# Turning the quantised weights on TensorE during attention instead of turning them in the DMA load

## The reference

```python
x = x + _L0_xattn_ref(_layernorm(x, axis=-1), ctx_768, Wq, Wk, Wv, Wo, bo)      # 8 heads of 64
x = x + _L0_ffn_ref(_layernorm(x, axis=-1), clip_x, clip_down, w_gate, w_up, w_down)

def _act_fake_quant(x, clip_factor):          # one scale for the whole tensor
    scale = jax.nn.sigmoid(clip_factor) * jnp.max(jnp.abs(x)) / 127.0
    return jnp.clip(round(x / scale), -128.0, 127.0) * scale
def _weight_fake_quant(w):                    # one scale for each row
    scale = jnp.max(jnp.abs(w), axis=1, keepdims=True) / 127.0
    return jnp.clip(round(w / scale), -128.0, 127.0) * scale
xq = _act_fake_quant(x, clip_x[0])
gate = xq @ _weight_fake_quant(w_gate).T      # w_gate, w_up: 1408 x 512
up = xq @ _weight_fake_quant(w_up).T
h = _act_fake_quant(silu(gate) * up, clip_down[0])
return h @ _weight_fake_quant(w_down).T       # w_down: 512 x 1408
```

## Time and profile before

| | |
|---|---|
| median of 3 runs | 570.46 us (569.67 to 570.75) |
| the profiled execution | 570.46 us, span of its profile 568.6 us |
| PE busy | 543.0 us, 95% |
| DVE busy | 471.8 us, 83% |
| ACT busy | 310.4 us, 55% |
| POOL busy | 233.9 us, 41% |
| DMA moved | 90.16 MB, mean 159 GB/s |

### The profile page before, as it was taken

One profiled execution on the slowest core, in us unless ns is written; L12 is line 12 of the kernel. 1 busy time (PEld: TensorE's weight loads), 2 busy tenths in 40 slices (PEclk: granted clock), 3 DMA queues, 4 the chain that ended last, 5 costly groups with the idle time before them and its releaser, 6 DMA issues.

```text
span 568.6 us, 8277 instructions
## 1 busy us (share of the span) xinstructions
PE 543.0 (95%) x2811; PEld 360.7 (63%) x2811; DVE 471.8 (83%) x874; ACT 310.4 (55%) x436; POOL 233.9 (41%) x352
## 2 busy tenths in 40 slices
PE   4999889999999999999899899999999999899997
PEld 2978678787888878787668544444444446443443
DVE  2747888989989888998987689889888988879883
ACT  3743546556464755544342666666666643999300
POOL 3576758679595968856342000000000000054442
PEclk9999999999999999999999999999999999999999
DMA  8708365756657573633295917541020010299887
GB/s 309 256 38 277 107 196 171 249 168 207 214 178 231 194 249 115 215 118 126 73 317 189 261 62 278 203 148 47 29 75 1 0 38 1 100 339 217 118 107 119
DMA packets 67779, 90.16 MB, mean 159 GB/s; under 512 B 32049, under 2 KB 34865, under 8 KB 67481
## 3 DMA queue, kind: packets, MB, share of 16 engines
q1 hardware_dynamic: 63413, 81.77, 44.6%
q0 software_dynamic: 4320, 7.87, 9.3%
q10 hardware_dynamic: 4, 0.00, 0.0%
HBM read 47.51 MB, written 37.78 MB: 150 GB/s over the span
## 4 chain that ended last, share of the span: by engine, by line
PE 50%; issue 34%; DVE 8%; DMA 5%; ACT 1%; POOL 1%; SPq 0%; POOLq 0%; DVEq 0%
PE QO L194 6%; PE QO L196 6%; PE QO L195 6%; PE SP L382 5%; PE WOP L495 4%; PE WOP L493 4%; PE WOP L494 4%; DMA out<-n2b 2%; PE PTP L1082 2%; PE PTP L430 2%; PE QO L1082 2%; PE SP L1082 2%; DMA wkr<-in_xattn_Wk 2%; PE MI L1082 1%; PE WOP L1082 1%
## 5 line engine op out<-in xcount | busy, mean ns | idle before, releaser
L45 POOL DMA_DIRECT2D out<-n2b x30 | 30.2, 1039 | 219.1 <-DVE n2b L1093 219.1
L977 PE MATMUL QO<-nT,wgu 128*128 128x512 bf16 x352 | 90.3, 379 | 0.6 <-ACT nT L221 0.6
L977 PE MATMUL SP<-nT,wgu 128*128 128x512 bf16 x352 | 90.3, 379 | 0.0
L983 ACT ACTIVATE sil<-QO,fsc 128x512 f32<-128x512 f32 x88 | 60.5, 687 | 50.7 <-PE QO L977 45.4
L987 DVE SCALAR_TENSOR_TENSOR h<-SP,fsc,sil 128x512 f32<-128x512 f32 x88 | 65.9, 749 | 14.9 <-PE SP L977 14.7
L422 POOL TENSOR_TENSOR PN<-P,rs 128x512 f32<-128x512 f32 x64 | 44.2, 712 | 57.8 <-DVE rs L414 57.8
L405 ACT ACTIVATE P<-P,r 128x616 f32<-128x616 f32 x32 | 26.0, 812 | 69.5 <-DVE P L401 69.5
L990 DVE TENSOR_REDUCE hmx<-h 128x1 f32<-128x512 f32 x88 | 60.4, 686 | 3.0
L977 PEld LDWEIGHTS SP<-nT,wgu 128*128 128x128 bf16 x352 | 34.4, 98 | 41.5
L977 PEld LDWEIGHTS QO<-nT,wgu 128*128 128x128 bf16 x352 | 33.2, 98 | 35.4 <-ACT nT L221 0.7
L194 PE MATMUL QO<-xTs,wqs 128*128 128x512 f32 x128 | 52.0, 407 | 1.8 <-DVE xTs L225 1.3
(11 more groups left out here) (169 smaller groups left out, 1162.9 us busy)
## 6 DMA issues: line engine op xcount, KB each, us to landing
xTr<-in_xT SPq DMA_DIRECT2D x8, 1024.0 KB, 8.0
xn<-in_x SPq DMA_DIRECT2D x32, 256.0 KB, 3.8
out<-x SPq DMA_DIRECT2D x32, 256.0 KB, 2.9
n_rows<-n SPq DMA_DIRECT2D x32, 256.0 KB, 2.6
n2b<-n_rows SPq DMA_DIRECT2D x32, 256.0 KB, 4.2
out<-n2b POOLq DMA_DIRECT2D x30, 256.0 KB, 4.4
h_spill<-h SPq DMA_DIRECT2D x2, 2816.0 KB, 9.3
h<-h_spill SPq DMA_DIRECT2D x6, 768.0 KB, 7.8
```

The costliest lines, as they stand in the source:

```text
L977: m = e.matmul(ps, wv_[:, k, col:col + 128], nT[:, b % 2, k, :], start=(k == 0), stop=(k == 3))
L983: t_sil[n] = add("act", lambda e: e.activation(sil[:, n % SR, :], gp, ACT.Silu, scale=fsc[:, ic:ic + 1]), [t_g[n], t_fs, t_h.get(n - SR)] ...
```

## The change

The weights are turned by TensorE during attention, and the two loads become plain ones.

- GpSimd's `wint` has one buffer where it had two, so `w_integer(i)` waits for the turning of tile i-1.
- `w_turn(i)` is new: TensorE transposes the 4 blocks of a tile (11 of a large one) into MI, in bf16; blocks 8 to 10 of a large tile go into the second bank of PTP. It waits for `w_integer(i)`, for the copy of the tile before (`t_we["last"]`), and for a large tile for the last reader of PTP.
- `w_out(i)` is new: ScalarE copies the turned blocks from PSUM to `wstg` (two buffers), in one instruction for a small tile and two for a large one; SP stores `wstg` to `wgud` or `wdd`, which now have the layout of `wgu` and `wd`. A store consists of 512 (large: 1408) pieces of 256 bytes, where it had 128 pieces of 1024 (2816) bytes.
- Tile i is turned at step i+2: a small one at the end of the step (before the query share that closes a step with t = 3), a large one, always at a step with t = 2, between `wo` and `PT`.
- The ring `P` of the softmax has 2 buffers where it had 3.
- The load of `wgu` is a plain DMA, added after step 31; the load of `wd` stays where it is and is plain.

```diff
-        wgud = dram("wgu_ints", (2 * I, D), bf16)
-        wdd = dram("wd_ints", (D, I), bf16)
+        wgud = dram("wgu_ints", (128, 4, 2 * I), bf16)
+        wdd = dram("wd_ints", (128, NI, D), bf16)
...
-        UR = 3
+        UR = 2
...
-        wint = sb(late, "wint", [128, 2, I], bf16)
+        wint = sb(late, "wint", [128, I], bf16)
+        wstg = sb(late, "wstg", [128, 2, NI, 128], bf16)
...
+            t_wb[i] = add("pool", lambda e: e.tensor_scalar(wint[:, 0:n * 128], v, -MAGIC, 1.0, ALU.add,
+                                                            ALU.mult), [t_wy[i], t_wt.get(i - 1)], "w_int")
+        MIb = MI[:, :].bitcast(bf16)
+        PTb = PTP[:, :].bitcast(bf16)
+        def w_turn(i, n):
+            nb = w_row(i)[1]
+            dst = [(MIb if k < 8 else PTb)[:, (k if k < 8 else k + 2) * 128:][:, 0:128] for k in range(nb)]
+            def fn(e):
+                for k in range(nb):
+                    m = e.transpose(dst[k], wint[:, k * 128:k * 128 + 128], identB[:, :])
+                return m
+            t_wt[i] = add("pe", fn, [t_wb[i], t_idB, t_we.get("last")] + ([t_pl[n - 1]] if nb > 8 else []),
+                          "w_tr")
+        def w_out(i, n, part):
+            nb = w_row(i)[1]
+            src, k0, k1, t = ((MIb[:, 0:1024], 0, min(nb, 8), None),
+                              (PTb[:, 1280:1664], 8, nb, t_PT.get(n) if nb > 8 else None))[part]
+            t_we["last"] = add("act", lambda e: e.activation(
+                wstg[:, i % 2, k0:k1, :], src[:, 0:(k1 - k0) * 128].rearrange("p (k c) -> p k c", c=128),
+                ACT.Copy), [t_wt[i], t, t_ws.get(i - 2)], "w_ev")
+            if part == 1:
+                return
+            at = W_ORDER[i]
+            out_ = wgud[:, :, at * 128:at * 128 + 128] if at < 22 else wdd[:, :, (at - 22) * 128:(at - 21) * 128]
+            t_ws[i] = dma("sp", out_, wstg[:, i % 2, 0:nb, :], [t_we["last"]], f"st_w{i % 2}")
...
+            if on["turn"] and not big:
+                w_turn(s - 2, s)
+                w_out(s - 2, s, 0)
...
-            t = add("pe", fn, t_dgs, "sd_mm")
+            t = add("pe", fn, [*t_dgs, t_we["last"]], "sd_mm")
...
-                t_wgu = c.dma_turn(wgu[:, :].rearrange("p (k n) -> p k n", k=4), wgud,
-                                   [t_qh[7, 3], t_ws[24], t_ws[25]], "ld_wgu")
             if s == 31:
-                gone = [t_S[31], t_q[7]]
+                gone = [t_S[31], t_q[7], t_ws[24], t_ws[25]]
+                t_wgu = dma("sp", wgu[:, :], wgud.rearrange("p k n -> p (k n)"), gone, "ld_wgu")
...
-        t_wdl = c.dma_turn(wd[:, :, :], wdd, flown + [t_g1, t_sdb, t_ws[24], t_ws[25]], "ld_wd")
+        t_wdl = dma("sp", wd[:, :, :], wdd, flown + [t_g1, t_sdb, t_ws[24], t_ws[25]], "ld_wd")
```

More of the change, by code:

```diff
@@ L37, in dma @@
         return self.add(engine, lambda e: e.dma_start(out, in_), waits, sig, 16)
-    def dma_turn(self, out, in_, waits, sig):
-        return self.add("sp", lambda e: e.dma_start_transpose(out, in_), waits, sig, 16)
     def dma_add(self, out, in_, waits, sig):
@@ L155, in block_kernel @@
         qs = sb(late, "qs", [128, 2, 4, 512])
-        wint = sb(late, "wint", [128, 2, I], bf16)
+        wint = sb(late, "wint", [128, I], bf16)
+        wstg = sb(late, "wstg", [128, 2, NI, 128], bf16)
         vbd = sb(late, "vbd", [128, 2, 5, 128], f32r)
         wraw = sb(late, "wraw", [128, 2, I])
-        sb(late, "unused1", [128, 88])
         os_ = sb(late, "os", [128, 2, 4, 512], f32r)
@@ L555, in block_kernel @@
         wd_v = w_down.rearrange("(r p) n -> r p n", p=128)
-        t_wr, t_wy, t_wb, t_ws, t_wiv = [Tokens() for _ in range(5)]
+        t_wr, t_wy, t_wb, t_wt, t_we, t_ws, t_wiv = [Tokens() for _ in range(7)]
+        t_we["last"] = None
         W_ORDER = [*range(22)]
@@ L595, in w_integer @@
             v = wraw[:, i % 2, 0:n * 128]
-            t_wb[i] = add("pool", lambda e: e.tensor_scalar(wint[:, i % 2, 0:n * 128], v, -MAGIC, 1.0, ALU.add,
-                                                            ALU.mult), [t_wy[i], t_ws.get(i - 2)], "w_int")
-            r = W_ORDER[i]
-            out_ = wgud[r * 128:r * 128 + 128, :] if r < 22 else wdd[(r - 22) * 128:(r - 21) * 128, :]
-            t_ws[i] = dma("sp", out_, wint[:, i % 2, 0:n * 128], [t_wb[i]], f"st_w{i % 2}")
+            t_wb[i] = add("pool", lambda e: e.tensor_scalar(wint[:, 0:n * 128], v, -MAGIC, 1.0, ALU.add,
[23 more added lines that the diff above has]
+            t_ws[i] = dma("sp", out_, wstg[:, i % 2, 0:nb, :], [t_we["last"]], f"st_w{i % 2}")
         for k in range(3):
@@ L650, in attend @@
             on = {"s": s + 1 < NT, "x": s + 3 < NT, "wo": s >= 5, "n2": s >= 6, "am": s >= 7, "w": 1 <= s < 27,
-                  "pv": t == 0 and b >= 1}
+                  "turn": 2 <= s < 28, "pv": t == 0 and b >= 1}
+            big = on["turn"] and w_row(s - 2)[1] > 8
             def when(key, fn, *args):
@@ L661, in turned @@
             def turned():
+                if big:
+                    w_turn(s - 2, s)
                 PT(s)
+                if big:
+                    w_out(s - 2, s, 1)
                 PT_high(s)
+                if big:
+                    w_out(s - 2, s, 0)
             if s < 26 and s != 2:
```

## The result

The changed kernel takes 577.96 us (median of 4 runs, 577.78 to 578.28); before, run beside it, takes 570.29 us (4 runs, 569.67 to 570.75). The ratio is 1.0125, with a 95% interval of 1.0106 to 1.0142: slower by 7.7 us. The profiled execution took 576.65 us (span 574.7), against 570.46 (span 568.6) before: 6.1 us longer in span. The four are on the high side: over all 21 executions of the changed kernel on record beside this result, the profiled one among them, the median is 577.57 us (575.74 to 578.86), some 7.3 us over before.

The account below looks back on a forecast made before the run. The prediction took TensorE to bound the kernel from 77 to 259 us. It added 7.6 us of paid turnings to 570.46 and took off 0.46 for a hole: 577.6 us, range 574.6 to 583.6.

Parts of the forecast that it names:

- 0.055 us of surcharge a tile: Attention: half of the 0.10 to 0.11 us by which f32 matmuls start slower behind a turning, added per tile.
- 18 small tiles are paid: Attention, tiles 2 to 23: 18 small tiles at 0.22 + 0.055 lengthen the kernel by 4.95 us.
- -0.46 for the hole at 208.68: TensorE's only hole between 77 and 259 us, behind an xn load, vanishes as TensorE is later: -0.46 us.
- Tiles 0, 1, 24 and 25 are hidden: Turned before 77 us or behind 259 us, ahead of TensorE's holes, these four tiles cost nothing.
- ScalarE's copies are hidden: Copies out of PSUM in attention, at most 20 us over 200: taken 0, at worst 0.2 us a batch.
- The turning loads give back nothing: Removing the two turning loads gains 0, as nobody waited for them; at most 3.2 us from 281 to 321.
- The small stores cost nothing, bounded below: Stores in 256-byte pieces: at most 1.0 us of all engines for a small one, 2.7 a large; taken 0.
- rival 2: Small stores delay the xn load VectorE needs first, 1 us for each of 6 batches: 583.6 us; chance 0.08.
- From 259 us on every stage has its old length: Expected sign: behind 259 us, after the stretch that TensorE bounds, no stage gets longer or shorter.
- the f32 price: Rival: transposes between attention's f32 matmuls cost what the f32 ones cost, 12.8 us in all: 582.8 us; chance 0.11.
- the whole duration: Rival: each of 132 transposes costs its whole duration of 0.219 us, 28.9 us in all: some 599; chance 0.02.
- not slower: Rival: VectorE sets the batch, turnings are hidden, waits from 281 to 321 us go: 567.2 us; chance 0.05 for a gain.

Follow-up runs that it names:

- e8_few_late_copy: e1_few_turns with ScalarE's copy of the staged tile moved behind q's product in each block's fourth step; 573.08 us, ratio 1.0050.
- e3_turn_twice: The changed kernel with every transposition made twice into the same place, 132 more; 585.28 us, ratio 1.0267.
- e9_turn_t3: e8_few_late_copy with seven more tiles turned, those of each block's fourth step; 574.56 us, ratio 1.0076.
- e11_first_and_late: The changed kernel, small tiles turned ahead of softmax transpositions in a block's first three steps, ScalarE's fourth-step copy behind q's product; 576.58 us, ratio 1.0120.
- e1_few_turns: The changed kernel with only tiles 0 and 4 turned; all copies, small stores, plain loads and buffers stay; 573.5 us, ratio 1.0061.
- e2_plain_loads: The kernel before with its two turning loads made plain ones of the same bytes at the same places; 570.3 us, ratio 1.0007.
- e7_small_stores: The kernel before with its 26 stores in 256-byte pieces and both loads plain, nothing turned on TensorE; 570.18 us, ratio 1.0008.
- e0_again: The changed kernel run and profiled once more, unchanged; 578.44 us, ratio 1.0145.
- e6: The changed kernel with small tiles turned ahead of the softmax transpositions in a block's first three steps; 576.9 us, ratio 1.0121.
- e10: e8_few_late_copy with six more tiles turned, those of each block's second step; 574.01 us, ratio 1.0073.
- e4_fill: The changed kernel with 14 idle matmuls ahead of tile 30's scores and 7 ahead of the down stage's third block; 577.6 us, ratio 1.0130.

## Why the prediction was right, point by point

The forecast was 577.6 us, and 577.96 was measured. The mechanism was right. That the sum came out so close is luck in part: the term of the small tiles was some 1.8 us too large, and some 2.6 us in the down stage and in the medians were not in the sum at all. The range's lower end is 574.8 by its own terms, not 574.6.

- **TensorE bounds the kernel from 77 to 259 us.** Right. TensorE is busy 33.00 of 33.00 us there after. Taking the turnings away takes 1.1 us a block of four tiles away (e8_few_late_copy), and doubling them adds their distance (e3_turn_twice).
- **0.22 us a small tile, 0.605 a large one.** Right: 0.19 to 0.23 and 0.63 in the timeline, 1.29 us a block for 23 doubled transpositions. The prediction says that the trace agrees as a duration with the 275 ns that it quotes. It does not quite: the median is 219 ns in both kernels, a fifth less.
- **0.055 us of surcharge a tile.** Right for small tiles of the first and second steps (0.23 to 0.29 us a tile in all, by the blocks); none behind the large ones, which stand between the last product of `wo` and the softmax transpositions (0.63 for a forecast 0.66).
- **18 small tiles are paid.** This is the step that was mis-sized. One in four stands in the gap of 0.26 us in front of q's product and costs nothing (e9_turn_t3). From step 5 to step 25, 20 tiles, before and after differ by 253.80 - 84.34 - (249.18 - 84.54) = 4.82 us: 11 small ones x 0.277 + 4 large ones x 0.63 = 5.6, less the 0.7 of the next point. The forecast has the same 20 tiles at 16 x 0.275 + 4 x 0.66 - 0.46 = 6.6. The gap could have been read from before: two starts, 164.37 and 165.18, 0.81 us apart with 0.55 us of work between.
- **-0.46 for the hole at 208.68.** Right in kind, and a little more: that block took 33.47 us before and its neighbours 32.8, so 0.67 came back.
- **Tiles 0, 1, 24 and 25 are hidden.** Tiles 0 and 1 are: after is even 0.20 us earlier at step 5. Tile 24 is not: the shift is 4.62 us at step 25, 4.88 at step 26 (tile 23, which was counted as paid) and 5.15 at step 27, and that last 0.27 is tile 24. Tile 25 adds nothing (5.12 at the scores of tile 30). The hole of 1.95 us in front of these came with them unchanged, because what ends it is VectorE, which is late by as much as TensorE was.
- **The turnings wait for nobody.** Right: between 77 and 262 us TensorE has no idle time after. The other way round GpSimd waits once, 2.28 us at 265.02, for a tile to be turned before it may write the one `wint` again, where the prediction had TensorE 1 to 5 us ahead at every step; no idle time of TensorE follows from it.
- **ScalarE's copies are hidden.** Right in the changed kernel (e11_first_and_late), with the margin where it was put: at q's copy, and only as long as TensorE is late. With few turnings it costs 0.33 us a block (33.14 us in e1_few_turns, 32.81 in e8_few_late_copy).
- **The turning loads give back nothing.** Right: 570.3 against 570.0 (e2_plain_loads); the plain load was in place 16 us early. It took 11.2 us to land where a transfer of the same size took 9.3.
- **The small stores cost nothing, bounded below.** Right for the size of the pieces (e7_small_stores). The prediction didn't see that the first large store moves into the burst in front of a load of x. In these traces TensorE stands idle for 0 to 1.4 us behind that load, once, not six times as rival 2 had it; that the store is the cause is not shown.
- **From 259 us on every stage has its old length.** Not so in time, though no work was added there. From the scores of tile 30 (5.1) the shift grows to 5.6 at the gate stage, 0.5 for the stretch at half the clock in this execution. It is 5.4 just ahead of the idle time in the third block of the down stage and 6.1 behind it, 0.7 for TensorE's wait there.

That last wait is VectorE's, for a slot that an accumulating store of the output frees. The timeline of DVE in after:

```profile
520.64 0.69 DVE L1133 TENSOR_TENSOR n2b<-QO,sdb 128x512 f32<-128x512 f32 x1 [1.78 <-DMA out<-n2b]
```

And in before:

```profile
514.53 0.69 DVE L1093 TENSOR_TENSOR n2b<-QO,sdb 128x512 f32<-128x512 f32 x1 [0.59 <-DMA out<-n2b]
```

TensorE's hole behind it is 0.28 us in before, 0.20 in e7_small_stores and none in e2_plain_loads. It is 0.90 to 1.25 in the five traces in which every tile is turned and nothing fills the hole (0.98 in after, 1.12 in e0_again, 0.90 in e3, 0.95 in e6, 1.25 in e11), and 0.72, 0.76, 0.56 and 0.28 in e1, e8, e9 and e10, which turn few but have the staged stores. So it is not the staged stores alone, since e10 has before's 0.28 with them, though the instructions of that stage are the same in all. Each kernel has one trace, and the same kernel differs by 0.14 in two. Why the stores land later is open.

So the 7.7 us are made up of 5.1 that are there at the scores of tile 30 and are TensorE's own, some 0.7 in the down stage, and some 1.9 that are in the medians and only in part in the profiled execution, where a stretch at half the clock makes 0.5 of them. By the median of all 21 executions it is 1.5 in place of 1.9. Candidates for the rest are the late load of step 8 and such stretches in other places. In e8_few_late_copy, with two tiles turned (0.9 us by price), the median is 3.0 us over before. Its profiled execution, the fastest of six at 571.71, is 1.2 us longer in span than before's; so 1.4 to 1.8 of the 3.0 come from executions that no trace shows. Its mean clock doesn't sort its executions: the three with a mean clock of 0.997 or 0.998 take 572.7 us on average, the three with 0.999 or 1.000 take 572.9. So for this kernel the stretches at half the clock don't explain it. What does is open.

Of the rivals, the f32 price (582.8) falls by the block, which would have been over 34.9 us even with the free tile, and the whole duration (599) with it. Each transposition's duration is what it was in the gate stage, by its line in after (ns min/median/max, first and last start):

```profile
L607 PE MATMUL MI<-identB,wint x120: 217/219/230, 61.2 to 269.3; 128*128 128x128 bf16 x120
```

That the change is not slower (567.2) falls twice. The loads had nothing to give (e2_plain_loads), and VectorE waits for TensorE longer than before, 1.89 us where the earlier trace rows have 1.61. The timeline of DVE in after:

```profile
162.60 0.69 DVE L515 TENSOR_TENSOR x<-WOP,xn 128x512 f32<-128x512 f32 x1 [1.89 <-PE WOP L491]
```

The Trainium skill, "VectorE: DVE Perf Modes", section "The three transpose paths", has the DMA path far dearer for one block than TensorE. As a rule for where to put the work it failed here: the path that it has as the dearer one cost this kernel 0 us (e2_plain_loads), and the cheaper one 5.

## What to carry to other kernels

Price an operation on the engine that sets the pace by the distance at which its neighbours follow it, and take the DMA's hidden time as worth nothing: 132 transpositions of 0.055 us on the full engine cost more than 11 us of a queue that nobody waited for. Before multiplying a price by a count, subtract the starts of the rows around each place and compare with the work between them: a gap that matmul ends cover in the timeline (0.26 us a block here) makes a quarter of the places free. When work is taken off the pacing engine or put on it, look at which copies of other engines were hidden by its lateness, and which stores move with the new work, and into which burst.

## What the runs showed of the hardware that was not expected

- Four bf16 transpositions of 128 x 128 between f32 products cost what they cost between bf16 ones (0.22 us): 0.19 to 0.23 us, and a whole turning 0.02 to 0.05 us more by the blocks in most places.
- After an idle time of about 1 to 2 us, TensorE ran at half its clock for a few microseconds in some executions, and in others of the same kernel it did not: granted clock 0.81 over 9 us in after, 1.00 in e0_again. With products on ones in those holes the profiled execution (e4_fill) shows no such stretch, but another of its four has a mean clock of 0.996, and the medians gained nothing.
- A load of 2816 KB held SP's queue for 0.33 us as a plain transfer and for 10.75 as a turning one, and freeing the queue was worth nothing (e2_plain_loads).
